# Four PSUM banks regrouped as two pairs of banks in the first attention of a two-layer kernel

## The reference, cut to what matters

```python
xn = layernorm(x)
q = (xn @ Wq).reshape(B, S, 16, 64)          # 16 heads of 64
k = (c @ Wk); v = (c @ Wv)                   # regrouped by head
scores = einsum(q, k) * 64 ** -0.5           # per batch and head: 256 x 1601
scores = where(all(c == 0), -inf, scores)
att = softmax(scores)                        # over the 1601 context rows
x = x + (att @ v) @ Wo
```

## Time and profile before

| | |
|---|---|
| median of 3 runs | 2168.86 us (2168.7, 2168.86, 2173.09) |
| span of the profiled execution | 2168.4 us |
| PE busy | 2030.2 us (94%), 10757 matmuls |
| PEld busy | 1431.6 us (66%) |
| DVE busy | 1710.2 us (79%) |
| ACT busy | 1073.8 us (50%) |
| POOL busy | 1163.8 us (54%) |
| mean granted TensorE clock | 0.969 of full speed |

### The profile page before, as it was taken

One profiled execution on the slowest core, in us unless ns is written; L12 is line 12 of the kernel. 1 busy time (PEld: TensorE's weight loads), 2 busy tenths in 40 slices (PEclk: granted clock), 3 DMA queues, 4 the chain that ended last, 5 costly groups with the idle time before them and its releaser, 6 DMA issues. The chain is left out here.

```text
span 2168.4 us, 35171 instructions
## 1 busy us (share of the span) xinstructions
PE 2030.2 (94%) x10757; PEld 1431.6 (66%) x10757; DVE 1710.2 (79%) x4048; ACT 1073.8 (50%) x1493; POOL 1163.8 (54%) x624
## 2 busy tenths in 40 slices
PE   5999999999999999999999999999986899859995
PEld 4666666666666666666666666666654688647774
DVE  7788878878887888888888878878756777767764
ACT  3445445453535455454535445454533699744442
POOL 0275755657475756656575656557674354314340
PEclk9899999999999999999999999999996999979997
DMA  3000000000000000000000000000000121022210
GB/s 94 1 1 16 1 3 4 14 1 4 18 1 1 4 16 1 3 18 1 1 4 16 1 4 1 1 1 1 1 0 21 60 88 58 25 76 62 61 46 23
DMA packets 54855, 40.84 MB, mean 19 GB/s; under 512 B 2500, under 2 KB 51596, under 8 KB 53644
## 3 DMA queue, kind: packets, MB, share of 16 engines
q1 hardware_dynamic: 54668, 38.57, 6.0%
HBM read 37.45 MB, written 1.11 MB: 18 GB/s over the span
## 5 line engine op out<-in xcount | busy, mean ns | idle before, releaser
L374 POOL TENSOR_TENSOR a_den<-a_den,a_probs 128x1024 f32<-128x1024 f32 x352 | 846.7, 2408 | 362.8 <-ACT a_probs L571 362.7
L571 ACT ACTIVATE a_probs<-a_probs,a_mask_col 128x1024 f32<-128x1024 f32 x416 | 478.9, 1151 | 578.6 <-DVE a_probs L740 578.5
L740 DVE TENSOR_TENSOR a_probs<-a_scores,a_shift 128x512 f32<-128x512 f32 x832 | 566.8, 686 | 180.1 <-PE a_scores L399 162.3
L681 DVE CUSTOM_DVE_ANT_0 a_work<-a_work,a_mask_row 128x400 f32<-128x400 f32 (+1 forms) x1024 | 572.7, 587 | 35.6 <-PE a_work L431 33.2
L479 PE MATMUL a_pv<-a_probs,a_V 128*64 128x256 f32 x3328 | 451.0, 392 | 5.8 <-ACT a_outT L578 3.8
L431 PE MATMUL a_work<-a_cT_hi,a_Q_hi 128*128 128x400 f32 (+1 forms) x1024 | 357.5, 380 | 2.6
L397 PE MATMUL a_scores<-a_Q_hi,a_cT_hi 128*128 128x512 f32 x832 | 340.5, 409 | 0.1
L398 PE MATMUL a_scores<-a_Q_lo,a_cT_hi 128*128 128x512 f32 x832 | 327.9, 394 | 0.0
L399 PE MATMUL a_scores<-a_Q_hi,a_cT_lo 128*128 128x512 f32 x832 | 326.5, 392 | 0.0
L479 PEld LDWEIGHTS a_pv<-a_probs,a_V 128*64 128x64 f32 x3328 | 202.5, 136 | 186.0 <-issue 116.3
L431 PEld LDWEIGHTS a_work<-a_cT_hi,a_Q_hi 128*128 128x128 f32 x1024 | 194.9, 190 | 137.1 <-issue 89.6
(11 more groups left out here) (319 smaller groups left out, 2855.9 us busy)
## 6 DMA issues: line engine op xcount, KB each, us to landing
m_gate_rows<-gate_scratch SPq DMA_DIRECT2D x8, 1024.0 KB, 4.7
a_c_nat<-in_ctx_dram SPq DMA_DIRECT2D x8, 768.0 KB
b_c_in<-in_ctx_dram SPq DMA_DIRECT2D x8, 768.0 KB
b_c_nat<-in_ctx_dram SPq DMA_DIRECT2D x8, 768.0 KB
m_w_raw<-in_L_ffn_W_dram SPq DMA_DIRECT2D x16, 256.0 KB, 5.0
a_acc<-in_x_dram SPq DMA_DIRECT2D x8, 128.0 KB, 2.0
out_dram<-tokens SPq DMA_DIRECT2D x4, 256.0 KB, 2.3
a_V<-in_L_xattn_Wq_dram SPq DMA_DIRECT2D x1, 512.0 KB, 6.8
```

The costliest lines, as they stand in the source:

```text
L374: nc.gpsimd.tensor_tensor(half, so_far, probs[:, buffer(c, j), :], ALU.add).then_inc(den_added, 1)
L571: nc.scalar.activation(probs[:, buffer(c, j), :], probs[:, buffer(c, j), :], ACT.Exp, bias=mask_col[:, c // 2 % 2, j // 2:j // 2 + 1]).the ...
L681: nc.vector.tensor_tensor_reduce(out=X[:, bank, :w], in0=X[:, bank, :w], in1=mask_row[:, off:off + w], scale=1.0, scalar=-3e38, op0=ALU.ad ...
L740: nc.vector.tensor_tensor(probs[:, buffer(c, j), pair * 2 * S:(pair + 1) * 2 * S], Sc[:, pair, :], shift[:, first:first + 2 * S], ALU.add) ...
```

## The change

The four banks become two pairs (`PAIRS = 2`). An item now takes a pair: it waits until item n-2 has been read out, PE fills both banks, one semaphore step tells the readers, and they read up to 1,024 columns in one instruction. There are half as many items of each kind: cT with 8 chunks and cxT with the other 5, two masks, two q items of four heads, seven v items (six of two chunks), 32 max items of two matmuls of 402 columns, two spreads, and one den item. PE issues as many matmuls as before. The new instructions of DVE are the same operations at up to twice the width. The positions are rewritten as well: den is in slot 5, right behind the P·V of step 1; the v items stand after max items 0, 2, 4, 6 and 12 and in slots 95 and 100; both halves of the first spread are in slot 92, those of the second in slot 98.

```diff
-    PIECES = [(0, 402), (402, 400), (802, 400), (1202, 400)]
+    PIECE = 402
+    HALF = 2 * PIECE
     UNITS = G8 * 2
-    BANKS = 4
-    TAIL = 3
-    V_AFTER = [1, 4, 6, 8, 10, 12, 14, 26, 38]
-    LATE_V = [95, 97, 100, 102]
+    PAIRS = 2
+    TAIL = 2
+    V_AFTER = [0, 2, 4, 6, 12]
+    LATE_V = [95, 100]
     MAX_END = 92
     SHIFTS = [83, 93]
     DIAG = [84, 88]
-    SPREAD = [92, 93, 98, 99]
+    SPREAD = [92, 98]
...
-            early += [("cT", i) for i in range(3)] + [("cxT", 3)] + [("mask", i) for i in range(4)]
-        early += [("q", i) for i in range(4)]
-        vs = [("v", c) for c in range(NC)]
-        for u in range(UNITS * 4):
+            early += [("cT", 0), ("cxT", 1)] + [("mask", i) for i in range(2)]
+        early += [("q", i) for i in range(2)]
+        vs = [("v", c) for c in range(0, NC, 2)]
+        for u in range(UNITS * 2):
             early.append(("max", u))
...
-            slots[3].append(("den", 0))
-            slots[7].append(("den", 1))
+            slots[5].append(("den", 0))
...
-        X = es.enter_context(nc.psum_tensor("a_work", [P, BANKS, 512], F32))
+        X = es.enter_context(nc.psum_tensor("a_work", [P, PAIRS, 2, 512], F32))
...
         def taken(eng, it, use):
-            eng.wait_ge(bank_free[use % BANKS], at(it, PER_TURN // BANKS, use // BANKS + 1))
+            eng.wait_ge(bank_free[use % PAIRS], at(it, PER_TURN // PAIRS, use // PAIRS + 1))
...
# tensor engine, in item()
-                bank, s = use % BANKS, c + 1
-                if use >= BANKS:
-                    taken(pe, it, use - BANKS)
-                out = X[:, bank, :]
+                bank, s = use % PAIRS, c + 1
+                if use >= PAIRS:
+                    taken(pe, it, use - PAIRS)
+                out = X[:, bank, :, :].rearrange("p h n -> p (h n)")
...
                 elif kind == "mask":
-                    pe.wait_ge(flag_done, at(it, 8, s // 2 * 4 + i + 1))
+                    pe.wait_ge(flag_done, at(it, 4, s // 2 * 2 + i + 1))
...
                 elif kind == "max":
-                    off, w = PIECES[i % 4]
-                    last = nc.tensor.matmul(out[:, :w], Q[s % 2][0][:, i // 4 * P:(i // 4 + 1) * P],
-                                            cT[s // 2 % 2][0][:, off:off + w], start=True, stop=True)
+                    for k in range(2):
+                        off = (i % 2 * 2 + k) * PIECE
+                        last = nc.tensor.matmul(X[:, bank, k, :PIECE], Q[s % 2][0][:, i // 2 * P:(i // 2 + 1) * P],
+                                                cT[s // 2 % 2][0][:, off:off + PIECE], start=True, stop=True)
...
                 elif kind == "den":
-                    pe.wait_ge(den_added, at(it, 4 * (STEPS - 2), c * (STEPS - 2) - 1 + i))
-                    for k in range(2):
+                    for k in range(4):
+                        if k % 2 == 0:
+                            pe.wait_ge(den_added, at(it, 4 * (STEPS - 2), c * (STEPS - 2) - 1 + k // 2))
                         for odd in range(2):
...
# scalar engine, in item()
                 elif kind == "v":
-                    nc.scalar.activation(V[:, s % 2, i, :], X[:, bank, :], ACT.Copy).then_inc(bank_free[bank], 1)
+                    n = min(2, NC - i)
+                    nc.scalar.activation(V[:, s % 2, i:i + n, :], X[:, bank, 0:n, :], ACT.Copy)\
+                      .then_inc(bank_free[bank], 1)
...
# vector engine, in item()
                 elif kind == "max":
-                    off, w = PIECES[i % 4]
                     filled(dve, it, use)
                     dve.nop(nofuse=True)
-                    nc.vector.tensor_tensor_reduce(out=X[:, bank, :w], in0=X[:, bank, :w],
-                                                   in1=mask_row[:, off:off + w], scale=1.0, scalar=-3e38,
+                    masks = mask_row[:, i % 2 * HALF:(i % 2 + 1) * HALF].rearrange("p (h n) -> p h n", h=2)
+                    nc.vector.tensor_tensor_reduce(out=X[:, bank, :, :PIECE], in0=X[:, bank, :, :PIECE],
+                                                   in1=masks, scale=1.0, scalar=-3e38,
                                                    op0=ALU.add, op1=ALU.max, accum_out=maxes[:, s % 2, i:i + 1])\
                       .then_inc(bank_free[bank], 1)
```

More of the change, by code:

```diff
@@ L149, in prep_slots @@
             slots[DIAG[i]].append(("diag", i))
-        for i in range(4):
+        for i in range(2):
             slots[SPREAD[i]].append(("spread", i))
@@ L248, in attention_0 @@
         xn_all, wv_ready = sem("xn_all"), sem("wv_ready")
-        bank_full = [sem(f"bank{i}_full") for i in range(BANKS)]
-        bank_free = [sem(f"bank{i}_free") for i in range(BANKS)]
+        bank_full = [sem(f"pair{i}_full") for i in range(PAIRS)]
+        bank_free = [sem(f"pair{i}_free") for i in range(PAIRS)]
         hi_done = sem("hi_done")
@@ L426, in item @@
                 elif kind == "v":
-                    last = split_product(out, cT[s // 2 % 2], Wv, slice(i * P, (i + 1) * P),
-                                         slice(s % 2 * G8 * HD, (s % 2 + 1) * G8 * HD))
+                    for k in range(min(2, NC - i)):
+                        last = split_product(X[:, bank, k, :], cT[s // 2 % 2], Wv, slice((i + k) * P, (i + k + 1) * P),
+                                             slice(s % 2 * G8 * HD, (s % 2 + 1) * G8 * HD))
                 elif kind == "max":
-                    off, w = PIECES[i % 4]
@@ L433, in item @@
                 elif kind == "spread":
-                    if i < 2:
-                        pe.wait_ge(diag_done, at(it, 32, 8 * s + 4 * (i + 1)))
-                    else:
-                        pe.wait_ge(shift_steps, at(it, 20, 5 * s + 5))
-                    last = nc.tensor.matmul(out, ones_r[:, :], shift_diag[:, i % 2 * 4:i % 2 * 4 + 4, :], start=True, stop=True)
+                    for k in range(2):
+                        if i == 0:
+                            pe.wait_ge(diag_done, at(it, 32, 8 * s + 4 * (k + 1)))
+                        elif k == 0:
+                            pe.wait_ge(shift_steps, at(it, 20, 5 * s + 5))
+                        last = nc.tensor.matmul(X[:, bank, k, :], ones_r[:, :], shift_diag[:, 4 * k:4 * k + 4, :],
+                                                start=True, stop=True)
@@ L522, in _ @@
             stages(pe, body)
-            for n, kind in enumerate(("den", "den", "proj")):
-                item(None, STAGES, kind, n % 2, first_use(STAGES) + n)
+            for n, kind in enumerate(("den", "proj")):
+                item(None, STAGES, kind, 0, first_use(STAGES) + n)
         @block.scalar
@@ L608, in _ @@
             copy_outT(None, STAGES, 1)
-            for i in range(2):
-                item(None, STAGES, "den", i, first_use(STAGES) + i)
+            item(None, STAGES, "den", 0, first_use(STAGES))
         @block.vector
@@ L701, in item @@
                         dve.wait_ge(shift_steps, at(it, 20, 5 * s + 4))
-                        for quarter in range(2):
-                            filled(dve, it, prep_use(it, c, "spread", quarter))
+                        filled(dve, it, prep_use(it, c, "spread", 0))
                         nc.vector.tensor_tensor(shift_diag[:, :, :],
@@ L708, in item @@
                 elif kind == "recip":
[L709 to L710 removed]
+                    if i == 0:
+                        taken(dve, it, use_of(the_plan(it, c), "den", 0))
                     part = rden[:, i * P:(i + 1) * P]
@@ L730, in subtract @@
                     if j < 2:
-                        for quarter in (2 * j, 2 * j + 1):
-                            taken(dve, it, prep_use(it, c - 1, "spread", quarter))
+                        taken(dve, it, prep_use(it, c - 1, "spread", j))
                     if c > 0 or j > 3:
@@ L774, in _ @@
             taken(dve, None, last)
-            taken(dve, None, last + 1)
             for i in range(8):
@@ L778, in _ @@
                 nc.vector.reciprocal(part, part).then_inc(recip_done, 1)
-            item(None, STAGES, "proj", 0, last + 2)
+            item(None, STAGES, "proj", 0, last + 1)
 def moe_0(nc, gate_w, w1, b1, w2, b2, ws1, bs1, ws2, bs2, XS, ident):
```

85 lines of the change are left out of this document (43 added, 42 removed).

## The result

The changed kernel takes 2179.78 us (median of 5, 2179.0 to 2181.92); the kernel before 2172.89 us in 5 runs (2168.7 to 2173.11). The ratio is 1.0038, 95% interval 1.0025 to 1.0051: slower, by 0.4%. The medians differ by 6.9 us and the spans of the two profiled executions by 8.9 (2177.3 against 2168.4). The prediction had the sign and the place right, and the size too small: 5.6 us more than before were forecast, and the first attention alone is 10.2 us longer in the profiled executions. The untouched blocks behind it took 1.3 us less (from the first layer norm of the next block to the end 533.07 us, before 534.41), which no part of the change explains; over all the runs of this study that stretch lies between 529 and 538 us.

A forecast was written before the change was run, and what follows sets the result against it. The prediction took PE to bound the stages and DVE's readout to set the prologue's time. From a span of 2168.4 us it added 6.5 for the prologue, −1.3 for the stages and 0.4 for the tail: 2174.0 us, range 2166 to 2181.

The forecast's parts named there:

- Stages bound by PE, DVE's saving hidden: In the stages PE sets the time, so the 3.8 us of DVE time saved per stage is off the path.
- The wide maximum at 1.01 us: One DVE instruction reading a pair takes 1.01 us, saving 0.12 us of fixed cost per pair.
- rival D: The wide maximum isn't faster per column: 2.9 us more in the prologue, 2177 us; chance 0.55 together with the main forecast.
- The excursions, −0.7 a stage: Den behind P·V saves two switches to 64-column tiles in each of 14 stages: 0.7 us each, −9.8 us.
- Waits in front of masks and den: PE waits in stages: 0.67 us at the first mask, 0.36 at den in odd stages; 0.55 at den in even ones.
- The spread, taken at 0 out of 0 to 0.3: At a stage's end the first spread waits for diag and a pair: 0 to 0.3 us, taken as 0.
- The prologue: Main term, before the first scores: every item waits for the item before the last; +6.5 us, bounds +2 and +10.
- part 2: Prologue's V items: four cycles of a V pair and two wide maxima, 3.29 us each; ninth pair starts 4.9 us later.
- part 3: Prologue's other 24 pairs at 1.05 us each plus a V pair of 2.4 us; last readout ends near 82.4.
- A: Rival: the wide instruction pays in the prologue, which stays about even, and stages keep 6 to 7 us; 2163 us, chance 0.12.
- B: Rival: the two sides cancel, prologue +2.5 to +3 us, stages −2 to −4; 2168.6 us, chance 0.20.
- C: Rival: a new stall over 0.5 us in every stage, plus a prologue at 1.2 GHz throughout (+10); 2185 us, chance 0.13.

The follow-up runs named there:

- den third: The kernel after, with each stage's third early item (first mask or first maximum) moved from slot 4 to slot 6, behind den: 2177.03 us, ratio 1.0031.
- V apart: The kernel after, with V's matmuls in the prologue going to P·V's two idle banks, so V holds no working pair: 2174.59 us, ratio 1.0014.
- the extra matmuls: The kernel after, with unread matmuls of 512 columns ahead of some waits for a pair in the prologue: 2172.92 us, ratio 1.0011.

## Why the prediction was right or wrong

**Stages bound by PE, DVE's saving hidden.** Right for the kernel before. For the kernel after it is half right: with pairs, narrow maxima cost 0.2 to 0.8 us a stage. The forecast had no term for this, and needed none, as the change has the wide ones.

**The wide maximum at 1.01 us.** Right (0.997), and rival D falls.

**The excursions, −0.7 a stage.** Right in even stages (−0.71, shown apart with four banks), mis-sized in odd ones: −0.3 there.

**Waits in front of masks and den.** Right in place. By start to start the mask is 0.8 us late (forecast 0.67), den in odd stages 0.38 (0.36) and in even ones 0.54 (0.55). The flags were done 5.0 us after the first transposes, as forecast (185.05 to 190.02): the scan began later than reckoned, the low part lasted 1.22 us as reckoned, and the flags 0.68 where 0.95 was taken. PE was there at 4.25 us, not 4.4.

**The spread, taken at 0 out of 0 to 0.3.** Mis-sized: 0.14 at its second matmul and 0.12 at the P·V behind it in most odd stages, 0.25 us together. With 0.1 at the mask and 0.4 less from the excursions that would make the 0.8 us by which odd stages came out longer; but a part of the 0.4 is, in the run with four banks, itself a wait at the mask, so some of it may be counted twice, and this balance is not closed. Even ones gained 0.57 and not 0.15. These 0.4 us have no cause here: without the wait for Q's low part an even stage takes 95.03 us with pairs (den third) and 95.49 with four banks and den in slot 5, so something else in the order of the pairs saves 0.46 us. From first scores to last P·V the two nearly cancel, and +0.85 stands against −1.3: 2.2 us, the second mis-sized term of the sum after the prologue's.

**The prologue.** This is the step that failed, by 2.4 us out of 8.9, and it failed in part 2. The start (+1.5) and part 3 (55.93 to 84.72 is 28.8 us; forecast 28.9) and the end (4.95; 4.9) came as forecast. Part 2 reckoned four cycles of 3.29 us, 13.2 in all, with V's six matmuls at the full clock; they took 15.5. The text gave the low clock to part 3 and not to part 2, but in this execution V's first fill ran at 1.2 GHz and took 2.6 us instead of 1.4. By the two executions with 14.0 us that is 1.5 of the 2.3. The other 0.8 is the cycle itself: the first and the fourth take 3.7 us at the full clock too. In the first, V's fill begins 0.4 us later against the maxima, as it waits for Q's low part; for the fourth no cause is shown. That part 3 came out at the forecast value has some luck in it: in den third, with the same prologue and a clock of 0.55 instead of 0.66 from 65 to 85 us, it took 29.7 us, and the first scores came at 89.33 all the same, 2.0 us later than forecast. The bound of +10 held the true value, and the value taken in it was too low. Against after, V apart came to 6.5 us and the extra matmuls to 6.1, both together to 10.6. Against an execution with the same clock up to maximum 8, V's hold is worth 4.5 us (83.60 to 79.11) and the extra matmuls 5.7 (89.33 to 83.60).

**The tail.** +0.4 forecast, +0.5 measured.

**The rivals.** A fell: refill did not hide, and V's hold was as dear as was argued. B fell. C was right about two of its ingredients, the cold prologue and something at the spread, but no stage lost the 0.5 us on top that it asked for. The rule of the Trainium skill that matmul groups should rotate through PSUM banks so that readout overlaps (Perfetto Trace Analysis, Matmuls) agrees with what the prologue lost: with V in two more banks 6.5 us came back, 4.5 of them at a like clock.

## What to carry to other kernels

Halving the number of buffers to double the width of the readout can pay only where readout is the bound and the refill still hides. No run here shows such a stretch: the even stages came out shorter, but for a reason that wasn't found. An item that is long to fill and long to read (V here) then stops everything behind it. When you reckon such a cycle, work it out at both levels of the clock: waits that the change itself makes can put PE at the lower one, and where that falls differs from one execution to the next. For the same reason, take the clock of a stretch from more than one execution before you call it an effect of an edit. And take a change apart before you keep it or throw it away: one line of this one, den behind P·V, was worth 0.3%, the rest cost more than that.

## What was unexpected in the hardware

TensorE's granted clock in a stretch in which it mostly waits is worth as much as the waits. In the prologue of after it averages 0.66 of full speed from 65 to 85 us, a mean of stretches at its two levels of 1.2 and 2.4 GHz. Useless matmuls ahead of the waits held it at 1.00 and brought the first scores 5.7 to 6.1 us earlier, though PE had more to do.

Where in the prologue the clock is low differs between executions of the same code. From 40 to 45 us it was 0.66 in after and 1.00 in den third, and in both PE had just waited for Q's low part (1.32 us, and 0.95 and 0.79). The total hardly changed (first scores at 89.67 and 89.33). What decides about the place, these runs do not show.
